# Second mixture-of-experts dispatch: order of statistics, routing and bias additions; gathers in pairs; one weight load a group later

## The reference

```
x = x + tanh(g_xattn[i]) * attention_i(layernorm(x), ctx)
x = x + tanh(g_ffn[i])   * ffn_i(layernorm(x))
```

```
xn = x * rsqrt(mean(x*x) + eps) * rms_w
scores = softmax(xn @ gate_w.T);  e = argmax(scores)
out = max(scores) * (silu(xn @ W1[e] + b1[e]) @ W2[e] + b2[e])
```

## Time and profile before

| | |
|---|---|
| median of 3 runs | 776.3 us (774.14 to 778.49) |
| profiled execution | 768.22 us, span 766.1 us |
| mean granted TensorE clock | 0.925 of full speed |
| busy share PE / DVE / ACT / POOL | 86% / 59% / 52% / 41% |
| `experts(1)`, from half 2's route to its first slot | 524 to 554 us |
| `experts(1)`, slots | 554 to 622 us |
| `heads8(1, 6)` and `ternary` | 622 to 766 us |

### The profile page before, as it was taken

The page is one execution under the profiler, slowest core; times in us unless marked ns, Lnnn a source line. Parts: engine busy times, 40 slices in busy tenths (PEclk is TensorE's granted clock), DMA queues, the critical chain, the costliest instruction groups (busy, mean ns, idle before and its releaser), DMA issues.

```text
span 766.1 us, 17361 instructions
## 1 busy us (share of the span) xinstructions
PE 660.2 (86%) x6445; PEld 552.0 (72%) x6445; DVE 450.2 (59%) x1400; ACT 399.3 (52%) x977; POOL 311.9 (41%) x266
## 2 busy tenths in 40 slices
PE   3698997879989899899999999784699868999894
PEld 2487775779989777688887854563489857777684
DVE  5375768732223668575656677655433335779693
ACT  4565542355546565465656567321155745666471
POOL 4654430826234276132232347402234447654041
PEclk9699998699999999999999999985599988999997
DMA  6643680856776210000000020003357653521001
GB/s 169 162 99 90 195 241 2 245 154 173 219 223 188 85 31 25 1 2 1 1 1 2 1 83 1 1 0 96 116 138 228 174 161 98 144 56 37 3 15 42
DMA packets 60716, 70.92 MB, mean 93 GB/s; under 512 B 7051, under 2 KB 40859, under 8 KB 60635
## 3 DMA queue, kind: packets, MB, share of 16 engines
...
## 4 chain that ended last, share of the span: by engine, by line
PE 65%; DVE 18%; POOL 6%; issue 4%; ACT 3%; DMA 3%; SPq 0%; POOLq 0%; ACTq 0%; DVEq 0%
PE banks L1475 9%; PE banks L1491 8%; PE banks L1609 4%; PE banks L1312 3%; PE banks L1201 3%; PE banks L1618 3%; PE banks L1629 3%; PE banks L1289 3%; PE banks L1159 3%; PE banks L1161 2%; PE banks L1160 2%; PE banks L1267 2%; PE banks L1301 2%; PE banks L1661 2%; DVE rr L1955 2%
## 5 line engine op out<-in xcount | busy, mean ns | idle before, releaser
L994 ACT ACTIVATE hT<-banks,wup 128x128 f32<-128x128 f32 x304 | 86.8, 369 | 72.1 <-PE banks L1475 71.9
L913 ACT ACTIVATE pT<-banks 77x512 f32<-77x512 f32 x128 | 69.1, 591 | 54.8 <-PE banks L1289 54.4
L719 POOL DMA_INDIRECT xs<-xn,slot x48 | 47.0, 979 | 100.0 <-DVE ysb L2273 50.1
L624 POOL TENSOR_TENSOR kbd<-k,const 96x1248 fp32r<-96x1248 f32 x32 | 72.8, 2285 | 32.7 <-PE banks L1289 30.2
L1475 PE MATMUL banks<-xTs,wup 128*128 128x128 f32 x608 | 83.7, 283 | 2.1 <-issue 2.1
L1491 PE MATMUL banks<-wd,hT 128*128 x608 | 81.8, 279 | 0.6 <-ACT hT L994 0.3
L1475 PEld LDWEIGHTS banks<-xTs,wup 128*128 128x128 f32 x608 | 77.3, 200 | 3.0 <-issue 2.7
L679 POOL TENSOR_TENSOR sh<-sh,rd 128x616 f32<-128x616 f32 x32 | 39.0, 1218 | 98.8 <-DVE rd L1912 98.7
L2273 DVE COPY ysb<-banks 128x128 f32<-128x128 f32 x76 | 22.1, 291 | 91.7 <-PE banks L1491 91.7
L1491 PEld LDWEIGHTS banks<-wd,hT 128*128 128x128 f32 x608 | 74.7, 194 | 1.3 <-issue 1.1
L604 POOL TENSOR_TENSOR rstd<-vv,const 128x4 f32<-128x4 f32 x24 | 25.5, 1061 | 112.1 <-DVE vv L1859 111.8
...
## 6 DMA issues: line engine op xcount, KB each, us to landing
...
q<-queries SPq DMA_DIRECT2D x21, 256.0 KB, 4.2
...
ys<-ysb SPq DMA_DIRECT2D x16, 256.0 KB
...
```

The costliest lines, as they stand in the source:

```text
L624: pool.tensor_tensor(kbd[b % NB8][0:96, :, :, :].bitcast(F32R), kb, m, ALU.mult).then_inc(h8.kbd, 1)
L719: pool.indirect_dma_start(xs[hh], bass.IndirectOffsetOnAxis(ap=idx[hh % 2][k_][:, t:t + 1], axis=0), xn8[hh % 2][:, t, :], None).then_inc( ...
L913: act.activation(pT[b % 2][0:SK, u, :], ps[0:SK, 2 + u % 2, :], ACT.Exp, scale=D8 ** -0.5)\
L994: ins = act.activation(hT[T % 3][:, c, :], ps[:, T % 2, c * P:c * P + P], func, bias=wup[T % NW][:, HID + c:HID + c + 1])
```

## The change

Nothing is computed that was not computed before; instructions and waits stand in another order, in run 1 (layer 2's experts and what follows) alone.

- DVE in `experts(1)`: the statistics of half 3 stand ahead of half 2's `route` and `slots`; `norm8(3, ..)` right after `slots(2)`, and `weigh(2)` behind it; `bias8(2, 0)` between `route(3)` and `slots(3)`; the two additions of `bias8` are separate calls now, one behind `slots(3)`, one in the loop over slots after the first `give`. `weigh(3)` and the bias of half 3 come one slot later in that loop.
- PE in `experts(1)`: `turn(3, ..)` and `logits(3)` first, then `second_bias(2)`, `ranks(3)`, `add_bias(2)`.
- POOL: `token_roots(3)` stands ahead of `spread(2)` and no longer between its third and fourth scatter. In `heads8(1, 6)` the eight gathers of half 3 are split: two, the masked keys of sequence 3, two; then the keys of sequence 4, then four.
- DVE in `heads8(1, 6)`: four tiles of half 3 are added at `b == 2`, the other four at `b == 4`.
- SP: the loads of `wfr`, `wpr`, `lnw` stand ahead of group 2's `query_roles` and no longer behind group 1's.

```diff
@@ -579,13 +579,13 @@
                 if g == 2:
                     store_keys(1, 3)
                 store_queries(1, g)
-                query_roles(1, g)
-                if g == 1:
+                if g == 2:
                     wait_done(sp, "ff", 2)
                     sp.wait_ge(h8.st, 4 * (B + GB))
                     sp.dma_start(wfr[:, :], a["fc"]).then_inc(ld.l3, 16)
                     sp.dma_start(wpr[:, :, :], a["proj"]).then_inc(ld.l3, 16)
                     sp.dma_start(lnw[:, :, :], a["ln"]).then_inc(ld.l3, 16)
+                query_roles(1, g)
             od = out.rearrange("b t d -> t b d")
             for g in range(NG):
                 sp.wait_ge(tn.x, g + 1)
@@ -642,7 +642,7 @@
             def heads8(run, phase):
                 rows = a_raw[:, 4 * P:5 * P]
                 for b in range(B):
-                    if b + 2 < B and (b or run == 0):
+                    if b + 2 < B and (b >= 2 or run == 0):
                         keys(run, b + 2)
                     if b == 0:
                         if run == 0:
@@ -651,7 +651,11 @@
                         pool.wait_ge(su.zero, 4 + 2 * run)
                         bias_rows(0, NG * phase, rows)
                         if run:
-                            collect(3)
+                            collect(3, 0, 4)
+                            keys(1, 3)
+                            collect(3, 1, 4)
+                    if run and b == 2:
+                        collect(3, 1, 2)
                     if b % GB == 1 and b // GB < NG - 1:
                         bias_rows(b // GB + 1, NG * phase + b // GB + 1, rows)
                     if run == 0 and b == 4:
@@ -708,8 +712,8 @@
                 for k_ in range(chosen(hh)):
                     for t in range(HT):
                         m = k_ * HT + t
-                        if hh % 2 == 0 and m == 3:
-                            token_roots(hh + 1)
+                        if hh == 0 and m == 3:
+                            token_roots(1)
                         if hh == 0 and m == 6:
                             length_roots(1)
                         if hh == 1 and m == 8:
@@ -782,6 +786,7 @@
             for g in range(0, NG - 1):
                 rsqrt_front(g + 4 * NG + 2)
             token_roots(2)
+            token_roots(3)
             spread(2)
             spread(3)
             wait_done(pool, "h1", 1)
@@ -1497,15 +1502,21 @@
                 if run == 0:
                     folded_weights(0)
                     folded_weights(1)
-                second_bias(hh)
-                add_bias(hh)
-                turn(hh + 1, 0)
-                turn(hh + 1, 1)
-                logits(hh + 1)
-                if run == 0:
+                if run:
+                    turn(hh + 1, 0)
+                    turn(hh + 1, 1)
+                    logits(hh + 1)
+                    second_bias(hh)
+                    ranks(hh + 1)
+                    add_bias(hh)
+                else:
+                    second_bias(hh)
+                    add_bias(hh)
+                    turn(hh + 1, 0)
+                    turn(hh + 1, 1)
+                    logits(hh + 1)
                     first_keys(range(0, 10))
-                ranks(hh + 1)
-                if run == 0:
+                    ranks(hh + 1)
                     first_keys(range(10, H))
                     pe.wait_ge(h64.q, H)
                 for i in range(3):
@@ -1528,9 +1539,9 @@
                             front(6 * NG)
                         if hh == 3 and i == 10:
                             queries(1, 6, 0)
-                        if h == 0 and i == 2:
+                        if h == 0 and i == 2 + run:
                             second_bias(hh + 1)
-                        if h == 0 and i == 4:
+                        if h == 0 and i == 4 + run:
                             add_bias(hh + 1)
                 pe.wait_ge(mo.ye, T + nt)
 
@@ -1996,7 +2007,10 @@
                     if b % GB == 0 and g < NG - 1:
                         query_lo(run, g + 1)
                     if b == 2 and between:
-                        between()
+                        between((0,), (0,))
+                        lk.wait()
+                    if b == 4 and between:
+                        between((0,), (1,))
                         wait_done(dve, "ff", 2)
                     if run and b in (6, 10, 11, 12, 14):
                         ternary_weights((6, 10, 11, 12, 14).index(b))
@@ -2175,11 +2189,11 @@
                     dve.wait_ge(mo.ct_mm, hh + 1)
                     dve.tensor_copy(cT[:, :, :].rearrange("p a t -> p (a t)"), ps[0:GB * E, 2, 0:2 * P]).then_inc(mo.ct, 1)
                 else:
-                    for i in range(2):
-                        dve.wait_ge(mo.b_mm, 2 * hh + i + 1)
-                        t0 = HT * (hh % 2) + GB * i
-                        xt = x[:, t0:t0 + GB, :].rearrange("p t d -> p (t d)")
-                        dve.tensor_tensor(xt, xt, ps[:, 2 + i, :], ALU.add).then_inc(mo.xb, 1)
+                    i = a_ - 1
+                    dve.wait_ge(mo.b_mm, 2 * hh + i + 1)
+                    t0 = HT * (hh % 2) + GB * i
+                    xt = x[:, t0:t0 + GB, :].rearrange("p t d -> p (t d)")
+                    dve.tensor_tensor(xt, xt, ps[:, 2 + i, :], ALU.add).then_inc(mo.xb, 1)
 
             def gate_lengths(part):
 
@@ -2231,25 +2245,33 @@
                 route = route_top1 if run else route_top2
                 weigh = weigh_top1 if run else weigh_top2
                 hh = 2 * run
+                wait_done(dve, "h1" if run else "h8", 1)
+                stats8(hh + 1, 0)
+                stats8(hh + 1, 1)
+                variance8(hh + 1)
                 if run:
                     for part in range(4):
                         route(hh, part)
                     slots(hh)
-                wait_done(dve, "h1" if run else "h8", 1)
-                stats8(hh + 1, 0)
-                stats8(hh + 1, 1)
-                variance8(hh + 1)
-                weigh(hh, gate)
-                bias8(hh, 0)
-                norm8(hh + 1, 0)
-                norm8(hh + 1, 1)
-                bias8(hh, 1)
-                if run == 0:
+                    norm8(hh + 1, 0)
+                    norm8(hh + 1, 1)
+                    weigh(hh, gate)
+                else:
+                    weigh(hh, gate)
+                    bias8(hh, 0)
+                    norm8(hh + 1, 0)
+                    norm8(hh + 1, 1)
+                    bias8(hh, 1)
+                    bias8(hh, 2)
                     for j in range(4):
                         folded_weights_lo(j)
                 for part in range(4):
                     route(hh + 1, part)
+                if run:
+                    bias8(hh, 0)
                 slots(hh + 1)
+                if run:
+                    bias8(hh, 1)
 
                 def take(T):
 
@@ -2304,12 +2326,15 @@
                             take(T + i + 3)
                         give(T + i, i)
                         if h == 0:
-                            if i == 0:
+                            if run and i == 0:
+                                bias8(hh, 2)
+                            if i == run:
                                 weigh(hh + 1, gate)
-                            if i == 2:
+                            if i == 2 + run:
                                 bias8(hh + 1, 0)
-                            if i == 5:
+                            if i == 5 + run:
                                 bias8(hh + 1, 1)
+                                bias8(hh + 1, 2)
                         else:
                             if run == 0 and i in (10, 11):
                                 combine(hh - 1, 0, i - 10)```

Some rows of the order in which instructions stand, as the built programs have them (line, operation, written tile and read tiles, size, and how many in a row; numbers behind names tell buffers apart).

DVE in `experts(1)`, behind the last instruction of `slots(2)` (`etile`). Before: the statistics `st`, `mv`, `vv` of half 3, then `weigh(2)` up to `cw`.

```order
L2169 TENSOR_SCALAR etile_103<-S_t 1x15
L2036 BN_STATS st_87<-x 128x6 x8
L2042 BN_AGGR mv_88<-st_87 128x2 x8
L2045 TENSOR_SCALAR vv_89<-mv_88 128x8
L2128 TENSOR_SCALAR rt<-rt 128x64
L2129 TENSOR_SCALAR rt<-rt 128x64
L2130 RECIPROCAL rt<-rt 128x64
L2131 TENSOR_TENSOR rt<-rt 128x64
L2132 TENSOR_REDUCE rs<-rt 128x8
L2133 RECIPROCAL rs<-rs 128x8
L2134 TENSOR_SCALAR share_92<-rs,tg 128x8
L2135 TENSOR_TENSOR cw_91<-rt,share_92 128x64
```

2 lines of the change are left out of this document (1 added, 1 removed).

## The result

The changed kernel takes 778.6 us in the median of 20 runs, the kernel before 774.9 us beside it: a ratio of 1.0041, with a 95% interval of 1.0024 to 1.0058. The change makes the kernel slower by 0.4%, where it had been forecast to make it faster by 0.7%.

A forecast was written before the change was run, and what follows sets the result against it. The prediction took the serial chain preparing `experts(1)` as the bound, then waits at the head of `heads8(1, 6)`. 5.5 + 0.2 = 5.7 us gain, 768.2 to 762.5 in the profile, median 776.3 to 770.5 us; range 766 to 775.5.

The forecast's parts named there:

- The preparation of `experts(1)`: Serial chain ahead of half 3's slots: first `take` at 547.7 us instead of 553.18, gain 5.5 us.
- The rows as last wait: Rival, 0.10: in `experts(1)` VectorE's work delays the scattered rows; gain only 1.4 us, 774.9 us.
- the rule against it: In `experts(1)`, VectorE operations using both ports would delay GpSimd's DMA descriptors; by the trace under 0.1 us a scatter.
- The clock: TensorE's clock in `experts(1)`: 0.50 up to the slots; 0.50 beyond 552 us would be wrong. Slower rival, 0.04.
- one rival: Rival, 0.12: sooner clock rise in the slots of `experts(1)`, 1.0 us, plus the full 1.6: gain 8.1, 768.2 us.
- The head of `heads8(1, 6)`: PE's waits for masked keys (0.59 us) and DVE (1.00) go: upper bound 1.6, kept 0.2, lower bound 1.1 lost.
- The additions at `b == 4`: In `heads8(1, 6)`, 1.09 us moved from `b == 2`, ahead of a reciprocal; exposed nearly in full with PE earlier.
- the gain is paid back behind: Rival, 0.10: late roots and masked keys, exposed additions in `heads8(1, 6)` cost 2.7 us; gain 2.8, 773.5 us.
- The POOL roots: In `heads8(1, 6)`, behind four gathers of 4.9 us: at about 652 us as before; later than 647 would be wrong.
- The loads of `wfr`: Behind half 3's last addition in `heads8(1, 6)`, at 663.6 us; landing near 668, 2 to 3 us early, cost 0.
- Profile and median: Whole kernel: profile 768.2 to 762.5 us, ratio 0.9926, carried to the median, 776.3 to 770.5 us.
- the eight scatters: Half 2's scatter in `experts(1)`: 9.8 us without the roots instead of 11.6, ending at 541.8.

The follow-up runs named there:

- dispatch part: Only the changes in `experts(1)`, with `heads8(1, 6)` and the loads of `wfr` as before, against the kernel before: ratios 0.9923, 0.9935 and 0.9947.
- e2: The changed kernel with `heads8(1, 6)` and the loads of `wfr`, `wpr`, `lnw` as in the kernel before: 769.8 us against 776.7, ratio 0.9923.
- e9: The kernel of e2 repeated on another chip: 763.3 us against 767.9 of the kernel before, ratio 0.9935.
- e15: The kernel of e2 repeated on a third chip: 770.9 us against 774.7 of the kernel before, ratio 0.9947.
- e10: The changed kernel, unchanged, on another chip: 768.0 us against 767.9 of the kernel before, ratio 0.9988.
- e16: The changed kernel, unchanged, on the chip of e15: 778.1 us against 774.7 of the kernel before, ratio 1.0061.
- e12: The changed kernel with the second four additions at `b == 3`, ahead of `normalise`: 763.1 us against 767.9 of the kernel before, ratio 0.9921.
- e5: e2 with the additions split and the loads of `wfr` placed as in the changed kernel, gathers whole: 766.6 us against 768.3 of the kernel before, ratio 0.9980.
- the second part: Only the changes in `heads8(1, 6)`, against the kernel before: ratio 1.0096 where the latter takes 776.7 us, 1.0048 where it takes 767.9.
- e13: The changed kernel with the second four additions at `b == 3`, behind `normalise(2)`: 775.3 us against 774.7 of the kernel before, ratio 0.9998.
- e4: The changed kernel with SP's keys of group 2 held back past the last gathers: 778.9 us against 776.7 of the kernel before, ratio 1.0028.
- the first profile: The profiled execution of the changed kernel from the first result, before the follow-up runs: 779.3 us.

## Why the prediction was wrong

- **The preparation of `experts(1)`: right.** 5.5 us were predicted. At the lower level, to which the profile that the prediction read belongs, 5.8 came in; at the upper 4.7, since DVE there starts half 3's route 1.05 us late (540.39, 541.44), beside the scatters. The dispatch part alone gained 6.9, 4.6 and 3.8 us on three chips (e2, e9, e15). Counted from the rows of `x`, which came 0.95 us late, each piece up to the logits is within 0.4 us, and the first `take` is 0.8 later than predicted. `second_bias(2)`, 0.44 us of PE between logits and ranks, was left out, and rightly costs nothing: PE is idle for 3.3 us behind it. Ranks were put at 1.4 us and took 1.13.
- **The rows as last wait: did not come.** From first to last scatter it is 8.99 us (532.84 to 541.83), 1.28 each, with `norm8` directly beside them. The rows were loaded at 544.11, and PE's transposes stood behind `add_bias(2)`. Of the rule against it nothing showed, as the prediction had read from the earlier trace rows.
- **The clock: right.** 0.50 up to the slots and 1.00 in them. It was still 0.50 from 552 to 553 us, which the prediction had named as a sign of being wrong; it rose from 553 on, 3.6 us after the first `take` (549.42), and in the trace before from 556 on, 2.8 us after it (553.18). So the gain that one rival expected from a sooner rise did not come.
- **The head of `heads8(1, 6)`: the step that failed.** The prediction kept "0.2 us of the 1.6" and gave as lower bound "the 1.1 us of additions lost with nothing gained". What was measured is a loss of 4.1 us by the ratios at the lower level (e10 against e9, 0.53%; 4.7 by the medians) and 8.8 at the upper (e16 against e15, 1.14%; 7.2 by the medians). Two terms were missing.
  - *The additions at `b == 4`.* The prediction took 1.09 us from the earlier trace rows for a group that had nothing of POOL beside it, and let it lie ahead of a reciprocal with 0.52 us of slack. In the new place POOL's masked keys of sequence 7 and its `bias_rows` run beside it: 3.45 us. And it stopped at the wait: the wait of 2.2 us also brings 1.2 GHz back for about 7 us. Together 5 us (0.67%, e10 against e12; e5 shows it with the gathers whole). This is half of the rival *the gain is paid back behind*, which had 10% and 2.7 us: its exposed additions came, its late roots and masked keys did not at the lower level (see the POOL roots below).
  - *The common stop.* At the upper level the second part costs 2.4 us (medians) to 4.7 us (ratios) more than at the lower. Kernels near each other say much the same: gathers in pairs with the additions at `b == 3` lose 4 us to the dispatch part at the upper level (e13 against e15, 0.51%) and nothing clear of noise at the lower (e12 against e9, -0.14%), but e13 has them behind `normalise` and e12 ahead of it. That the stop coincides with the last gathers is shown; what holds DVE and ACT back is not. The keys' traffic was excluded as its cause (e4), and busy DMA engines alone don't make it: in e10 their share is 1.07 from 640 to 644 us and nothing stops. Whether a signal between engines or an engine's next instructions came late was not tested. The cause stays open, and so does why the two levels differ in it.
- **The POOL roots.** The prediction expected them late because POOL would be busy with gathers. At the lower level that is what happened: in e10 they start at 646.81, right behind the last gather and with no idle time, 22.2 us after PE's first scores (22.5 before). In the first profile they came at 655.45 after POOL had idled 4.85 us: VectorE's statistics were late, not POOL.
- **The loads of `wfr`: hidden.** They were issued at 670.68 (prediction: 663.6, less the gain), 0.03 us after the addition they wait for, and DVE did not wait at 681.64.
- **Profile and median.** The prediction carried a ratio from a profile of 768.2 us over to a median of 776.3 us. That profile had no common stop in it, so nothing warned of one.
- **Small slips.** Without the roots the eight scatters take 9.95 us and not 9.8 (seven steps of 1.28 and the last instruction). Neither this nor rounding in the chain changes the sum by more than 0.2 us.

The best orders found are the dispatch part alone (0.9923 to 0.9947 on three chips) and, at the lower level only, the changed kernel with the second additions at `b == 3` (0.9921). The first beats the kernel before on each of its three chips, and the changed kernel wherever that ran beside it (e10, e16).
